# Gate branch of a quantised FFN clipped on GpSimd and quantised by a barrier of its own, `up` in eight PSUM banks

## The reference

```
x = x + xattn(layernorm(x), ctx)              # 32 query heads of 128, 4 key/value heads, softmax, output projection
h = act_qdq(layernorm(x))                     # the FFN from here
up   = act_qdq(h @ wu.T)                      # wg, wu, wd: weights in blocks of 32, 4 bits; 1376 features
gate = act_qdq(h @ wg.T)
sig  = fixed_qdq(sigmoid(gate), 1 / 65536)
gate = act_qdq(gate * sig)
o    = act_qdq(gate * up)
x    = x + o @ wd.T

act_qdq(a): mn, mx = min(a, 0), max(a, 0) over the whole tensor
            scale = (mx - mn) / 65535;  zp = round(-mn / scale)
            q = clip(round(a / scale) + zp, 0, 65535);  value (q - zp) * scale
```

## Time and profile before

| | us |
|---|---|
| median of 3 runs | 864.57 (863.89 to 865.39) |
| the profiled execution's own time | 863.88 |
| its span, first to last instruction | 862.1 |
| TensorE busy | 782.7 (91%) |
| VectorE busy | 628.7 (73%) |
| ScalarE busy | 454.9 (53%) |
| GpSimd busy | 250.8 (29%) |

### The profile page before, as it was taken

One profiled execution on the slowest core, in us unless ns is written; L12 is line 12 of the kernel. 1 busy time (PEld: TensorE's weight loads), 2 busy tenths in 40 slices (PEclk: granted clock), 3 DMA queues, 4 the chain that ended last, 5 costly groups with the idle time before them and its releaser, 6 DMA issues. The chain is left out here.

```text
span 862.1 us, 12646 instructions
## 1 busy us (share of the span) xinstructions
PE 782.7 (91%) x4746; PEld 465.3 (54%) x4746; DVE 628.7 (73%) x1141; ACT 454.9 (53%) x965; POOL 250.8 (29%) x382
## 2 busy tenths in 40 slices
PE   8998899999999999999999999997879999600998
PEld 3455466666666666666666666654334444200443
DVE  5873577788768778777788779986475489899741
ACT  5253456656556655566556555555140089495730
POOL 0210314356433466334455443442000012112000
PEclk9999999999999999999999999999989999955999
DMA  9121146756455575456664566997440000000000
GB/s 324 55 81 42 49 122 145 159 127 145 98 131 143 144 171 123 92 141 159 141 151 104 120 137 133 168 169 129 79 81 0 1 1 1 0 1 0 25 37 36
DMA packets 203437, 85.50 MB, mean 99 GB/s; under 512 B 170352, under 2 KB 186736, under 8 KB 203376
## 3 DMA queue, kind: packets, MB, share of 16 engines
q1 hardware_dynamic: 203376, 84.69, 43.1%
HBM read 31.72 MB, written 10.75 MB: 49 GB/s over the span
## 5 line engine op out<-in xcount | busy, mean ns | idle before, releaser
L314 PE MATMUL bank<-arena 128*128 128x256 f16 (+1 forms) x1872 | 261.0, 292 | 5.2 <-DVE arena L729 3.8
L314 PEld LDWEIGHTS bank<-arena 128*128 128x128 f16 x1872 | 182.8, 98 | 87.4 <-DVE arena L729 5.7
L1101 POOL TENSOR_SCALAR arena<-arena,rsum 128x256 f32<-128x256 f32 x256 | 133.7, 522 | 311.3 <-DVE rsum L793 297.3
L729 DVE SCALAR_TENSOR_TENSOR arena<-bank,arena 128x512 f16<-128x512 f32 x168 | 114.7, 688 | 118.1 <-ACT arena L541 117.7
L541 ACT ACTIVATE arena<-bank 128x512 f16<-128x512 f32 x168 | 98.7, 598 | 169.5 <-PE bank L414 93.9
L729 DVE SCALAR_TENSOR_TENSOR arena<-arena 128x512 f16<-128x512 f32 (+3 forms) x195 | 171.2, 889 | 15.3 <-ACT arena L541 14.7
L541 ACT ACTIVATE arena<-arena 128x512 f16<-128x512 f32 (+4 forms) x171 | 135.5, 813 | 61.7 <-POOL arena L1101 19.3
L583 ACT ACTIVATE arena<-bank,nmax 128x256 f32<-128x256 f32 x256 | 117.8, 472 | 60.0 <-DVE nmax L785 58.4
L428 PE MATMUL bank<-arena 128*128 128x512 f16 x512 | 122.4, 382 | 1.7 <-ACT arena L541 1.6
L484 PE MATMUL bank<-arena 128*128 128x512 f16 x528 | 116.7, 385 | 5.8 <-DVE arena L729 5.8
L404 PE MATMUL bank<-arena 128*128 128x256 f16 x768 | 94.3, 273 | 2.8 <-DVE arena L729 2.8
(11 more groups left out here) (87 smaller groups left out, 572.3 us busy)
## 6 DMA issues: line engine op xcount, KB each, us to landing
arena<-in_w_units SPq DMA_DIRECT2D x33, 256.0 KB, 3.6
w_ready<-arena SPq DMA_DIRECT2D x33, 256.0 KB, 3.3
arena<-in_wq SPq DMA_DIRECT2D x32, 256.0 KB, 3.5
arena<-in_wo SPq DMA_DIRECT2D x32, 256.0 KB, 3.6
arena<-in_x SPq DMA_DIRECT2D x1, 2048.0 KB, 15.1
out<-arena SPq DMA_DIRECT2D x8, 256.0 KB, 2.0
arena<-in_wk SPq DMA_DIRECT2D x4, 256.0 KB, 4.0
arena<-in_ctx_t SPq DMA_DIRECT2D x4, 256.0 KB, 4.6
```

The costliest lines, as they stand in the source:

```text
L314: last = nc.tensor.matmul(bank, a(i, c), b(j, c), start=start and c == 0 and n == 0, stop=stop and c == chunks - 1 and n == 2)
L729: return nc.vector.scalar_tensor_tensor(out=dst, in0=src, scalar=scale, in1=part, op0=ALU.mult, op1=ALU.subtract)
L1101: done = nc.gpsimd.tensor_scalar(p_s[:, t % 2, :, hh, :], p_s[:, t % 2, :, hh, :], rsum[:, t % 2, hh:hh + 1], P_SCALE, ALU.mult, ALU.mult)
```

## The change

1. **Five barriers in place of four.** QP gets a barrier of its own, put into VectorE's list between pieces 15 and 19 of `up`; QU's comes after piece 21. `constants` has four instructions up to `q_inv` instead of five.
2. **The barrier of QX without GpSimd.** TensorE transposes `worst`, VectorE reduces it and writes two values on a diagonal, TensorE multiplies ones by it, VectorE copies the result. The `keep_warm(14)` ahead of it becomes a `keep_warm(12)` behind it.
3. **GpSimd clips.** It clips the gate tiles and the sigmoid (both read int32), five tiles of QP (6 to 10) and nine of QU (2 to 10). ScalarE's L696, L707 and L709 are gone.
4. **`up` in eight banks** (`U_BANK`), and VectorE's order while `up` runs is written out anew.
5. **Behind `up`** ScalarE rounds `up` and two tiles of QP; nine of QP are rounded before the barrier QU. VectorE clips two tiles of QU, multiplies and takes the minimum.
6. **Down:** the first batch in three pieces (2, 3 and 6 tiles).

```diff
-P_ACT = range(5, 10)
-OQ_AT = (0, 5, FT)
+PC_DVE = range(0, 6)
+UC_DVE = range(0, 2)
+OQ_PIECES = [(0, 0, 2), (0, 2, 5), (0, 5, FT)] + [(b, *span) for b in range(1, B) for span in ((0, 5), (5, FT))]
+def U_BANK(n):
+    return (n + 4) % 8
...
             transpose_x2(B - 1)
-            keep_warm(14)
+            pe.wait_ge(worst_out, 1)
+            nc.tensor.transpose(banks[SC][0:2, 0:P], worst[:, 0, :], ident[:, :]).then_inc(x_turned, 1)
+            pe.wait_ge(ones_set, 1)
+            pe.wait_ge(x_diag, 1)
+            nc.tensor.matmul(banks[SC + 1][:, 0:2], ones[0:2, :], x_worst[0:2, 1:3], start=True, stop=True).then_inc(x_spread, 1)
+            keep_warm(12)
...
-            for t in range(4):
-                pe.wait_ge(g_free, 2 * FT + min(t, 2) + 1)
+            for n in range(2 * FT):
+                if n == 4:
+                    pe.wait_ge(g_free, 2 * FT + 3)
+                if n >= 8:
+                    pe.wait_ge(u_free, n - 7)
                 for c in range(HC):
-                    mm = ffn_part(1, 0, t, c)
+                    mm = ffn_part(1, n // FT, n % FT, c, U_BANK(n))
                 mm.then_inc(u_mm, 1)
-            ffn_tiles(1, 0, 4, u_mm, u_free)
-            ffn_tiles(1, 1, 0, u_mm, u_free)
...
+            gate_round(0)
+            gate_round(1)
...
+            for t in range(FT):
+                gate_sigmoid(t)
+                if t + 2 < FT:
+                    gate_round(t + 2)
             act.wait_ge(q_inv, 3)
+            for t in range(9):
+                p_rounded(t)
+            act.wait_ge(q_inv, 4)
             for t in range(FT):
-                rounded(up_i[:, t, :], up[:, t, :], QU).then_inc(u_round, 1)
-                rounded(gate_i[:, t, :], gate[:, t, :], QP).then_inc(p_round, 1)
-                if t in P_ACT:
...
+                u_rounded(t)
+                if t == 5:
+                    p_rounded(9)
+                if t == 6:
+                    p_rounded(10)
...
+            def constants(number, q, worth):
+                c, w, sign = qc[:, q, :], worst_all[:, 0, :], -1.0 if q == QP else 1.0
+                chain(nc.vector.tensor_scalar(c[:, 2:3], w[:, 0:1], w[:, 1:2], 1.0 / QMAX, ALU.add, ALU.mult))
+                chain(nc.vector.tensor_scalar(c[:, 3:4], c[:, 2:3], worth, 1e-12, ALU.mult, ALU.max))
+                chain(nc.vector.reciprocal(c[:, 4:5], c[:, 3:4]))
+                nc.vector.tensor_scalar(c[:, 6:7], c[:, 4:5], worth, sign, ALU.mult, ALU.mult).then_inc(q_inv, 1)
...
+            worst_of(QX, B)
+            dve.wait_ge(x_turned, 1)
+            nc.vector.tensor_reduce(x_worst[0:2, 0:1], banks[SC][0:2, 0:P], AX.X, ALU.max).then_inc(x_top, 1)
+            dve.wait_ge(x_top, 1)
+            nc.vector.tensor_scalar(x_worst[0:2, 1:3], ident[0:2, 0:2], x_worst[0:2, 0:1], None, ALU.mult).then_inc(x_diag, 1)
+            dve.wait_ge(x_spread, 1)
+            chain(nc.vector.tensor_copy(worst_all[:, 0, :], banks[SC + 1][:, 0:2]))
+            constants(1, QX, ones[:, 0:1])
...
++            gate_product(10)
+            dve.wait_ge(top_out, 2)
+            dve.wait_ge(gs_out, FT)
+            worst_of(QP, FT)
+            evacuate_up(16)
+            evacuate_up(17)
+            evacuate_up(18)
+            dve.wait_ge(worst_red, 2)
+            constants(3, QP, qc[:, QG, 10:11])
+            evacuate_up(19)
+            p_clipped(0)
+            p_clipped(1)
+            evacuate_up(20)
+            p_clipped(2)
+            p_clipped(3)
+            p_clipped(4)
+            evacuate_up(21)
+            dve.wait_ge(u_free, 2 * FT)
+            worst_of(QU, 2 * FT)
+            p_clipped(5)
+            dve.wait_ge(worst_red, 3)
+            constants(4, QU, qc[:, QX, 9:10])
...
+            def gate_clipped(t):
+                pool.wait_ge(g_round, t + 1)
+                nc.gpsimd.tensor_scalar(gate[:, t, :], gate_i[:, t, :], qc[:, QG, 7:8], qc[:, QG, 8:9], ALU.max, ALU.min).then_inc(g_clip, 1)
+            def sigmoid_clipped(t):
+                pool.wait_ge(sig_round, t + 1)
+                nc.gpsimd.tensor_scalar(sig[:, t % 4, :], sig_i[:, t % 4, :], QMAX, -1.0, ALU.min, ALU.mult).then_inc(sig_clip, 1)
...
             all_reduce(2)
+            pool.wait_ge(q_set, 2)
+            gate_clipped(0)
             for t in range(FT):
-                pool.wait_ge(sig_left, t + 1)
-                nc.gpsimd.tensor_scalar(sig[:, t % 4, :], sig[:, t % 4, :], 1.0, -QMAX, ALU.mult, ALU.add).then_inc(sig_clip, 1)
-            all_reduce(3, 2)
...
+                if t + 1 < FT:
+                    gate_clipped(t + 1)
+                sigmoid_clipped(t)
+            all_reduce(3)
             all_reduce(4)
+            pool.wait_ge(q_set, 4)
+            p_clipped(6)
+            p_clipped(7)
+            for t in range(2, FT):
+                u_clipped(t)
+                if 4 <= t <= 6:
+                    p_clipped(t + 4)
+            all_reduce(5)
```

More of the change, by code:

```diff
@@ L148, in build @@
         winv = small("winv", [P, 2, 16])
[L149 removed]
+        stats = small("stats", [P, 5, 2, 2 * FT + 1])
+        x_worst = small("x_worst", [P, 4])
         top = small("top", [P, 4])
@@ L529, in _ @@
                 for t in range(FT):
-                    if t in OQ_AT:
-                        pe.wait_ge(oq_lo, 2 * b + OQ_AT.index(t) + 1)
+                    for i, (batch, first, end) in enumerate(OQ_PIECES):
+                        if batch == b and first == t:
+                            pe.wait_ge(oq_lo, i + 1)
                     for m, (h, r) in enumerate(((0, 0), (0, 1), (1, 0))):
@@ L711, in oq_half @@
             def oq_half(i):
-                b, tiles = i // 2, slice(OQ_AT[i % 2], OQ_AT[i % 2 + 1])
+                b, first, end = OQ_PIECES[i]
                 act.wait_ge(oq_clip, i + 1)
-                hi(oq[:, 0, tiles, b * P:(b + 1) * P], up[:, tiles, b * P:(b + 1) * P], 0.5).then_inc(oq_hi, 1)
-            act.wait_ge(q_inv, 4)
-            for i in range(2 * B):
-                b, tiles = i // 2, slice(OQ_AT[i % 2], OQ_AT[i % 2 + 1])
-                rounded(up_i[:, tiles, b * P:(b + 1) * P], up[:, tiles, b * P:(b + 1) * P], QO).then_inc(oq_round, 1)
+                hi(oq[:, 0, first:end, b * P:(b + 1) * P], up[:, first:end, b * P:(b + 1) * P], 0.5).then_inc(oq_hi, 1)
@@ L720, in _ @@
+            act.wait_ge(q_inv, 5)
+            for i, (b, first, end) in enumerate(OQ_PIECES):
+                rounded(up_i[:, first:end, b * P:(b + 1) * P], up[:, first:end, b * P:(b + 1) * P], QO).then_inc(oq_round, 1)
                 if i >= 1:
                     oq_half(i - 1)
-            oq_half(2 * B - 1)
+            oq_half(len(OQ_PIECES) - 1)
         @block.vector
@@ L1046, in _, with p_clipped, u_clipped @@
-            dve.wait_ge(top_out, 2)
-            dve.wait_ge(u_free, 2 * FT + 3)
-            dve.wait_ge(gs_out, FT)
-            quantisers(3, [(QU, 2 * FT, qc[:, QX, 9:10]), (QP, FT, qc[:, QG, 10:11])])
-            def clips(t):
+            def p_clipped(t):
+                dve.wait_ge(p_round, t + 1)
+                clip(gate[:, t, :], gate_i[:, t, :], QP).then_inc(p_clip, 1)
+            def u_clipped(t):
                 dve.wait_ge(u_round, t + 1)
                 clip(up[:, t, :], up_i[:, t, :], QU).then_inc(u_clip, 1)
-                if t not in P_ACT:
-                    dve.wait_ge(p_round, t + 1)
-                    clip(gate[:, t, :], gate_i[:, t, :], QP).then_inc(p_clip, 1)
@@ L1058, in _, with top_product, evacuate_up @@
-            clips(0)
+            def top_product():
+                dve.wait_ge(top_step, 3)
+                nc.vector.tensor_scalar(top[:, 3:4], top[:, 3:4], -1.0, QMAX, ALU.mult, ALU.add).then_inc(top_out, 1)
+                dve.wait_ge(top_out, 1)
+                nc.vector.tensor_tensor(stats[:, QP, 0, 0:1], top[:, 3:4], top[:, 0:1], ALU.mult).then_inc(top_out, 1)
+            def evacuate_up(n):
+                evacuate(up, QU, n, u_mm, u_free, U_BANK(n))
+            evacuate_up(0)
+            evacuate_up(1)
@@ new lines, in _ @@
+            evacuate_up(2)
+            gate_product(0)
+            evacuate_up(3)
+            top_product()
+            evacuate_up(4)
+            gate_product(1)
+            evacuate_up(5)
+            gate_product(2)
+            evacuate_up(6)
+            gate_product(3)
+            evacuate_up(7)
+            evacuate_up(8)
+            gate_product(4)
+            evacuate_up(9)
+            gate_product(5)
+            evacuate_up(10)
+            gate_product(6)
+            evacuate_up(11)
```

240 lines of the change are left out of this document (104 added, 136 removed).

## The result

| | before | after |
|---|---|---|
| median, timed together (4 runs each) | 864.23 us (863.27 to 865.39) | **939.41 us** (938.91 to 940.84) |
| ratio, 95% interval | | 1.0873 (1.0857 to 1.0889) |
| span of the profiled execution | 862.1 | 937.1 |
| GpSimd busy | 250.8 | 379.4 |
| TensorE's mean granted clock | 0.966 | 0.932 |

The kernel became 8.7% slower. The forecast was 851.5 us, its range ended at 865, and slower had a chance of 0.15. The page of the kernel after begins like this: the span, the busy time of each engine, and the shares of the chain that ended last, by engine.

A forecast was written before the change was run, and what follows sets the result against it. Matmuls were taken to bound the kernel until 747 us, then a serial chain of waits from 749. `worst` of QO moving from 796.65 to 783.5 saves 13.1 us, from median 864.57 to 851.5; range 847 to 865.

The forecast's parts named there:

- the part on the gate branch: Gate clips, sigmoid and products while `up` runs: 1.05 us per GpSimd clip, one tile costing the shared port 3.24 us.
- the first rival: GpSimd clips slower than 1.05 us, at most 2.1, making products wait while `up` runs; 884 us at 2.1; chance 0.26.
- Barrier QX: Before the gate: a 2.2 us chain without GpSimd in place of 6.15 us, gaining 3.9 us.
- Clock: At the gate's start: TensorE idles only 1.2 us, so its clock stays up, winning 2.6 us.
- Code load back to clips: After the all-reduce of QG, GpSimd changes back to clip code, taken as 7.0 us.
- Product 10, QP and QU: Late in `up`: product 10 ends near 731.6, QP's load at 736.2, `worst` of QU at 746.1 against 749.1.
- Behind `up`: From QU to QO: ten clips two per product, 5 x 3.24 us, then four tiles; `worst` of QO at 783.5 against 796.65.
- QO's own load: Behind the last clip: code load ending at 780.3, covered by four tiles; up to 6 us would show without them.
- Down: Start of down: the small first piece is worth nothing, as 4.94 us of warm matmuls stay ahead of it.
- The clock at the start of gate: Rival: the clock falls anyway, 2.6 us lost again, 854.1 us; chance 0.07 together with late QU.
- the free port: Rival: GpSimd's clips slip in beside VectorE, the tail shortens by 7 us, 844.6 us; chance 0.05.
- The late QU: Rival: QP's barrier delays VectorE, QU stays at 749.1, the tail is 37.4 us, 854.5; chance 0.07 together with clock.

The follow-up runs named there:

- c1_no_clip: The kernel after with GpSimd's 36 clips replaced by multiply and add, still reading int32, the clipping left out: 851.24 us, ratio 0.9846 to the kernel before.
- b1_x_turned: The kernel before with only the barrier QX taken through TensorE and keep_warm(12) behind it: 857.58 us, ratio 0.9916.
- d1_uint16: The kernel after with ScalarE writing uint16 (Relu) and GpSimd using only multiply and add, meant to keep all computation: 851.47 us, ratio 0.985 to before.
- a1_float_in: The kernel after with all GpSimd clips reading float32 in place of int32, the rounding left out: 938.91 us, ratio 1.085 to before.
- a3_sig_float: The kernel after with only the sigmoid's clip reading float32, its rounding left out: 939.67 us in one run.

## Why the prediction was wrong

**The step that failed is one price.** It stands in the part on the gate branch and in the first rival: "GpSimd's 1024 columns are 1.05", taken from a row of L1174, which multiplies and adds, for an instruction that clips. Measured, alone: 3.65 for minimum and multiply, 3.77 for maximum and minimum. I bounded the unknown by what seemed to differ (int32, bounds from memory, contiguity) and took the ceiling of 2.1 from instructions that change type or read two tensors. That the operation differs was not among these. The code had a hint that I passed over: each tensor_scalar of GpSimd in the kernel before multiplies and adds or multiplies twice, and where a clip was wanted, it was built from two ScalarE Relus and a multiply-add. Rows of the same shape and engine were no evidence for another operation, and the ceiling was no ceiling.

The rival's model was right, though it stopped at a price of 2.1 and 884 us, and the chance of 0.14 beyond 1.54 rested on that ceiling. With 3.5 us for each 0.1 beyond 1.54 and a price of 3.75 it gives 864.6 + 77.4 = 942; the kernel is at 939.4.

The Trainium skill, GPSIMD Engine Reference, section Engine selection, was weighed there too: elementwise "add/mul/max" on GpSimd is about twice as slow, but one-input work "roughly line-rate". I had let the 1.05 bear out the second clause. For multiply and add it holds by these runs (1.05 against VectorE's 0.73); for a maximum and a minimum the measurement differs and decides: 3.77 against 0.73 is five times.

**The other steps, read from c1_no_clip**, whose trace is up to QX 0.5 us later than that of before:

- *Barrier QX:* the gate starts at 627.39, 2.9 us before the 630.32 of the earlier trace rows, or 3.4 with that 0.5; forecast 3.9. The short chain took 0.5 more. Counted from `worst` of QX, b1_x_turned has the same (3.4). In the kernel after it reads as follows (timeline, start us, us):

```profile
621.88 0.27 PE L490 MATMUL bank<-ident,worst 128*2 128x128 f32 x1
...
622.19 0.28 DVE L1010 TENSOR_REDUCE x_worst<-bank 2x1 f32<-2x128 f32 x1 [0.39 <-PE bank L490]
...
622.86 0.35 PE L493 MATMUL bank<-x_worst,arena 2*128 2x2 f32 x2 [0.71 <-DVE x_worst L1012]
...
624.45 1.34 ACT L676 ACTIVATE arena<-arena,qc 128x512 int32<-128x512 f32 x2 [1.77 <-DVE qc L990]
```

- *Clock:* right. The 528 matmuls of gate and `up` take 114.12 us in c1_no_clip and 116.70 in the kernel before: the 2.6 of the forecast. In these two stretches of the kernel after the clock is granted 1.00, where the earlier trace rows had 0.50 and 0.61 (the clock stands behind the five busy times, ahead of the DMA share and the GB/s):

```profile
632.00:634.00 2.00, 2.00 (x11) 0.88 (x9) 2.00 (x4) 1.91 (x4) 0.00 (x0) 1.00 1.22 204
634.00:636.00 2.00, 2.00 (x11) 0.89 (x10) 1.97 (x6) 0.02 (x1) 0.00 (x0) 1.00 0.16 35
```

- *Code load back to clips:* 7.46 and 7.22 in c1_no_clip, 6.9 in the kernel after; 7.0 was taken.
- *Product 10, QP and QU:* GpSimd's last clip of the phase is over by 729.2, 1.0 ahead of the forecast, and the all-reduce of QP starts 6.55 behind it, at 735.71; 6.0 and 736.2 were forecast. Product 10, however, ends at 734.9 instead of 731.6. Nine of VectorE's eleven products come while an instruction of GpSimd holds the port, and take 1.85 to 2.08 us for it. So VectorE still has pieces 16 to 18 to move, takes up QP's constants at 738.82 (736.8 was forecast), and `worst` of QU is out at 748.07; 746.1, and 0.5 for the shift, was forecast. In d1_uint16 only three products are held up (1.81 to 2.05). Product 10 ends at 730.7, the load is in series as the forecast had it, and `worst` of QU is out at 745.01, 1.1 before the forecast. The first line below is the ninth product in c1_no_clip, the second the all-reduce of QP in d1_uint16:

```profile
728.32 1.90 DVE L1046 CUSTOM_DVE_ANT_0 arena<-arena 128x1024 f32<-128x1024 f32 x1
...
735.29 0.37 POOL L1250 PARTITION_ALL_REDUCE worst_all<-worst  x1 [6.07 <-issue]
```

- *Behind `up`:* turns of 2.98 instead of 3.24, the load 7.2 instead of 7.0. `worst` of QO is out at 785.15; forecast 783.5 and 0.5. In d1_uint16 it is out at 783.30. QO's own load is covered. In the kernel after, where the last clips end together with the tiles, it isn't: the all-reduce starts 5.84 us behind the last clip, and the constants of QO wait 3.5 us for it in place of 0.55. The forecast had named that as what appears if the cover goes.
- *Down:* "4.94 us of warm matmuls unchanged" was wrong for this trace. They took 6.06 in c1_no_clip, with a granted clock of 0.73 between 788 and 792, where the kernel before has 0.95 between 799 and 803. The change is not shown to be the cause: the same 16 matmuls take 4.92 to 4.97 in some traces and 6.06 to 6.53 in others, and the idle time of TensorE ahead of them doesn't sort them. It is 49.69 us ahead of the 4.94 of the kernel before, and 49.74 ahead of 6.09 in b1_x_turned; 93.92 stands ahead of 4.92 in a1_float_in and of 6.53 in a3_sig_float. What decides how soon the clock comes back there stays open.

With the 0.5 of the shift, these misses (1.1 at QO, 1.1 in the warm matmuls) make c1_no_clip's profiled span 851.5, 2.5 above the 849.0 of the sum. The other three executions have 849.0 to 849.6. So the sum's agreement with the median, to 0.3 us, is better than its steps, and partly luck. Two small slips stand in its working. Product 0 at 699.5 and ten turns of 3.24 give 731.9 for product 10, not 731.6. And the bounds for the code load (-14.1 at 6 us, -11.1 at 8) count 1 us on one side and 2 on the other, without a reason given.

**The other rivals.** The clock at the start of gate and the free port are ruled out by c1_no_clip: the clock is 1.00, and the port is held. The late QU is not ruled out by it: `worst` of QU is 1.0 us earlier than in the trace of before (748.07 against 749.1), where the forecast had 3.0 and the rival none, so two thirds of the rival came true in that trace. In d1_uint16 it is 4.1 earlier, and the rival fails. The rest came from the tail, 37.1 us in c1_no_clip and 38.3 in d1_uint16 in place of 47.5, as both had it (37.4).

## What to carry to other kernels

A duration is a price for an operation, not only for a shape: before work moves to another engine, find a row of that engine with the same operations, or measure it where that engine is idle, for which a few extra instructions in an idle stretch are enough. On GpSimd keep to multiply and add in an instruction with scalars, and let ScalarE's Relu do the lower bound; the write to an unsigned type can serve as the upper one only once it has been seen to stop at the limit. And where the price of an unknown stands in for work that lies in series 36 times, the ceiling of the range has to come from something that can hold it.
